# Patch layers of a four-layer image network: the Fourier products cut into 64x64 quarters of the array, and the inverse products in three rounds

## The reference, cut to what matters

```python
t = jnp.einsum('bchw,oc->bohw', x, w_in)                 # 192 -> 192 channels
tp = t.reshape(b, hid, h // 8, 8, w // 8, 8)             # patches of 8x8 pixels
tf = jnp.fft.rfft2(tp, axes=(3, 5)) * fft_filter[None, :, None, :, None, :]
tp = jnp.fft.irfft2(tf, s=(8, 8), axes=(3, 5))
t = conv3x3_depthwise(tp.reshape(b, hid, h, w), w_dw)
x1, x2 = t[:, :hid // 2], t[:, hid // 2:]
out = jnp.einsum('bchw,oc->bohw', gelu(x1) * x2, w_out)  # 96 -> 192 channels
```

## Time and profile before

| what | us |
|---|---|
| three runs, median (lowest to highest) | 2561.39 (2560.28 to 2563.0) |
| the profiled execution's own time | 2555.05 |
| its span, first to last instruction | 2553.0 |
| PE busy in the span | 2232.7 (87%) |
| DVE busy | 1667.8 (65%) |
| ACT busy | 1305.3 (51%) |
| POOL busy | 1113.0 (44%) |

### The profile page before, as it was taken

How to read it: one execution, slowest core, us unless ns; L and a number is a source line. 1 busy time by engine, 2 the same in 40 slices (tenths; PEclk the granted TensorE clock), 3 DMA queues, 4 the chain that set the end, 5 groups by cost and what they waited for, 6 DMA issues and landing times. The chain is left out here.

```text
span 2553.0 us, 63276 instructions
## 1 busy us (share of the span) xinstructions
PE 2232.7 (87%) x22485; PEld 1652.4 (65%) x22612; DVE 1667.8 (65%) x3120; ACT 1305.3 (51%) x2719; POOL 1113.0 (44%) x1393
## 2 busy tenths in 40 slices
PE   0699997998999169999999999999968999789998
PEld 0575645786788047777777777777756656366563
DVE  5345585674575168888888888888863455734557
ACT  0245540084057147777777777777733454334543
POOL 0333150000000147878787878778743222432225
PEclk9999997999999579999999999999989999989999
DMA  8623395415523312222222222222235045950349
GB/s 207 176 78 69 85 330 155 119 31 208 171 41 122 112 42 60 59 59 59 58 60 56 61 56 62 55 61 57 59 87 157 2 89 153 310 165 15 79 123 317
DMA packets 305576, 272.33 MB, mean 107 GB/s; under 512 B 175534, under 2 KB 238798, under 8 KB 299162
## 3 DMA queue, kind: packets, MB, share of 16 engines
q1 hardware_dynamic: 294650, 256.15, 36.1%
q0 software_dynamic: 9280, 6.44, 2.1%
q10 hardware_dynamic: 1496, 7.63, 0.8%
HBM read 165.44 MB, written 81.46 MB: 97 GB/s over the span
## 5 line engine op out<-in xcount | busy, mean ns | idle before, releaser
L1664 DVE TENSOR_TENSOR l_scan_att<-l_scan_decay,l_scan_causal_scores 128x512 f32<-128x512 f32 x384 | 327.4, 853 | 64.2 <-ACT l_scan_decay L1633 64.0
L714 ACT COPY l_arena<-l_body_bank 128x384 f32<-128x384 f32 x192 | 141.3, 897 | 308.3 <-PE l_body_bank L591 308.3
L1627 ACT ACTIVATE l_scan_decay<-l_scan_cum 128x512 f32<-128x512 f32 x384 | 216.3, 597 | 34.4 <-PE l_scan_cum L1519 34.3
L1633 ACT ACTIVATE l_scan_decay<-l_scan_decay 128x512 f32<-128x512 f32 x384 | 227.8, 631 | 4.1
L810 DVE TENSOR_TENSOR l_freq<-l_body_bank,l_filter 128x512 f32<-128x512 f32 x144 | 99.6, 692 | 183.8 <-PE l_body_bank L604 183.8
L1644 ACT ACTIVATE l_scan_yw<-l_scan_y_by_channel,l_scan_norm_b,l_scan_norm_w 128x128 f32<-128x128 f32 x384 | 148.0, 456 | 127.8 <-PE l_scan_y_by_channel L1581 126.8
L1566 PE MATMUL l_scan_gate_projected<-l_scan_xr,l_wf 97*128 97x128 f32 (+1 forms) x1536 | 206.6, 284 | 1.3 <-DVE l_scan_xo L1719 1.2
L1597 PE MATMUL l_scan_gate_projected<-l_scan_yz,l_scan_wo 128*96 128x128 f32 x1536 | 198.5, 279 | 1.1 <-DVE l_scan_yz L1696 1.1
L1597 PEld LDWEIGHTS l_scan_gate_projected<-l_scan_yz,l_scan_wo 128*96 128x96 f32 x1536 | 170.9, 163 | 40.0 <-issue 29.6
L571 POOL TENSOR_TENSOR l_arena<-l_arena 96x512 f32<-96x512 f32 x96 | 122.7, 1278 | 167.2 <-ACT l_arena L779 162.5
L1484 POOL TENSOR_TENSOR l_scan_inter<-l_scan_inter,l_scan_xd 128x384 f32<-128x384 f32 x128 | 128.0, 1000 | 152.5 <-DVE l_scan_inter L1679 152.5
(11 more groups left out here) (193 smaller groups left out, 4995.4 us busy)
## 6 DMA issues: line engine op xcount, KB each, us to landing
l_scan_xc<-convolved_rows SPq DMA_DIRECT2D x128, 224.0 KB, 2.8
x_after<-l_arena SPq DMA_DIRECT2D x64, 384.0 KB, 4.8
l_arena<-x_after SPq DMA_DIRECT2D x64, 384.0 KB, 5.6
convolved_rows<-l_slots SPq DMA_DIRECT2D x48, 441.0 KB
l_conv_x_main<-x_after SPq DMA_DIRECT2D x64, 256.0 KB, 2.6
l_arena<-x_after SPq DMA_DIRECT2D x16, 1024.0 KB, 8.3
prepare_xt<-x SPq DMA_DIRECT2D x8, 1536.0 KB
l_arena<-x SPq DMA_DIRECT2D x32, 384.0 KB, 5.7
```

The costliest lines, as they stand in the source:

```text
L714: nc.scalar.copy(tA[:, b, :, j:j + 2].rearrange("p c q -> p q c"), bank[n % 4][:, 0:2 * C].rearrange("p (q c) -> p q c", q=2)).then_inc(t_ ...
L1627: nc.scalar.activation(decay[:, b % 2, 4 * g:4 * g + 4, :], cum[(b + g) % 2][:], ACT.Relu, scale=-1.0)\
L1633: nc.scalar.activation(group, group, ACT.Exp, scale=-1.0).then_inc(exp_done, 1)
L1664: nc.vector.tensor_tensor(att[:, b, 4 * g:4 * g + 4, :], decay[:, b % 2, 4 * g:4 * g + 4, :], causal[:, b % 2:b % 2 + 1, :].broadcast_to([ ...
```

## The change

The products are made on 64x64 quarters of the array. For the transform, the four quarters are (half h of the block's pixels) x (half c of the channels). Rows h feed bank h of a pair of banks, and columns c are the partitions on which the result lands, so that `freq` now holds the first 96 channels on partitions 0 to 63 and the last 96 on partitions 64 to 127, with the upper and the lower patches of a block side by side in the free dimension: [128, 96, 2 x 128]. A unit is 2 rounds of 4 products of 384 columns in place of 3 products of 512, in the bank pairs 4, 5 and 6, 7 in turn, and DVE filters it in 4 instructions of 384 columns in place of 3 of 512. The filter is loaded in two pieces in the new layout.

The inverse of a group is 3 rounds of 4 products of 512 columns in place of 6 products. A round fills banks 2 and 3 together, and waits for all copies of the round before. DVE and ACT make the same 6 copies each, two a round. In the loop the rounds stand apart: round 0, build(g + 1, 1), round 1, build(g + 2, 0), round 2, and so on DVE and ACT. `gelu`, `gate` and the turning of blocks use the first 128 columns of each channel's 256.

```diff
                 def transform(m):
                     b = m % 2
                     pe.wait_ge(t_copied, (m + 1) * HALF // 2)
-                    for p in range(3):
-                        n = m * 3 + p
-                        if n >= 4:
-                            pe.wait_ge(t_hat, n - 3)
-                        nc.tensor.matmul(bank[4 + n % 4][:], dft, tA[:, b, 64 * p:64 * (p + 1), :].rearrange("p c j -> p (c j)"),
-                                         start=True, stop=True).then_inc(transformed, 1)
+                    for r in range(2):
+                        n = 2 * m + r
+                        if n >= 2:
+                            pe.wait_ge(t_hat, 2 * n - 2)
+                        for c in range(2):
+                            for h in range(2):
+                                at, first = slice(64 * h, 64 * h + 64), CH * c + sets * r
+                                last = nc.tensor.matmul(bank[4 + 2 * (n % 2) + h][64 * c:64 * c + 64, 0:sets * HALF], dft[at, at],
+                                                        tA[at, b, first:first + sets, :].rearrange("p c j -> p (c j)"),
+                                                        start=True, stop=True)
+                        last.then_inc(transformed, 1)
...
-                def invert(g):
-                    for p in range(PIECES):
-                        n = g * PIECES + p
-                        if n >= 2:
-                            pe.wait_ge(own_top, n - 1)
-                            pe.wait_ge(own_low, n - 1)
-                        c = channels(g, p)
-                        nc.tensor.matmul(bank[2 + n % 2][:], idft, freq[:, c:c + 4, :].rearrange("p c n -> p (c n)"),
-                                         start=True, stop=True).then_inc(back, 1)
+                def invert(g, rounds=range(PIECES // 2)):
+                    for q in rounds:
+                        n = g * PIECES // 2 + q
+                        if n >= 1:
+                            pe.wait_ge(own_top, 2 * n)
+                            pe.wait_ge(own_low, 2 * n)
+                        for h in range(2):
+                            for c in range(2):
+                                at, first = slice(64 * c, 64 * c + 64), g * PAIR + 4 * q
+                                last = nc.tensor.matmul(bank[2 + c][64 * h:64 * h + 64, :], idft[at, at],
+                                                        by_slab[at, first:first + 4, :, h, :], start=True, stop=True)
+                        last.then_inc(back, 1)
...
                 for g in range(groups):
                     convolve(g)
+                    if g + 3 < groups:
+                        invert(g + 3, [0])
                     if g + 1 < groups:
                         build(g + 1, 1)
                     if g + 3 < groups:
-                        invert(g + 3)
+                        invert(g + 3, [1])
                     if g + 2 < groups:
                         build(g + 2, 0)
+                    if g + 3 < groups:
+                        invert(g + 3, [2])
...
-                def place(g):
+                def place(g, rounds=range(PIECES // 2)):
                     if g >= STRIPS:
                         dve.wait_ge(convolved, PIECES * (g - STRIPS + 1))
-                    for p in range(PIECES):
-                        n = g * PIECES + p
-                        dve.wait_ge(back, n + 1)
-                        nc.vector.tensor_copy(win[g % STRIPS][0:64, 4 * p:4 * p + 4, 0:NPC:2, 0:NPC],
-                                              bank[2 + n % 2][0:64, :].rearrange("p (c i j) -> p c i j", c=4, i=slabs))\
-                            .then_inc(own_top, 1)
+                    for q in rounds:
+                        dve.wait_ge(back, g * PIECES // 2 + q + 1)
+                        for c in range(2):
+                            first = PAIR * c + 4 * q
+                            nc.vector.tensor_copy(win[g % STRIPS][0:64, first:first + 4, 0:NPC:2, 0:NPC],
+                                                  bank[2 + c][0:64, :].rearrange("p (c i j) -> p c i j", c=4, i=slabs))\
+                                .then_inc(own_top, 1)
...
-            nc.sbuf_tensor(f"{name}_freq", [128, C, H // SLAB * NPC], F32) as freq, \
+            nc.sbuf_tensor(f"{name}_freq", [128, CH, 2 * (H // SLAB) * NPC], F32) as freq, \
...
-        loads = list(pair_loads(arena, flat, 0)) + [(fsym[:], k["filters"][name]), (wi[:, 0], p["w_in"][0:128])]
+        loads = list(pair_loads(arena, flat, 0)) + [(wi[:, 0], p["w_in"][0:128])]
         loads += [(wi[64 * s:64 * (s + 1), 1], p["w_in"][128:C]) for s in range(2)]
+        loads += [(fsym[64 * s:64 * (s + 1)], k["filters"][name][64 * s:64 * (s + 1), CH * s:CH * (s + 1)]) for s in range(2)]
```

More of the change, by code:

```diff
@@ L438, in patch_body @@
     tA = arena[:, n_x:n_x + 2 * n_t].rearrange("p (b c j) -> p b c j", b=2, c=C)
-    by_slab = freq.rearrange("p c (i j) -> p c i j", i=slabs)
+    by_slab = freq.rearrange("p c (i h j) -> p c i h j", i=slabs, h=2)
+    sets = CH // 2
     strips = [arena[:, b * STRIP:(b + 1) * STRIP] for b in range(STRIPS)]
@@ L553, in _ @@
                     pool.wait_ge(rounded, 3)
-                pool.wait_ge(transformed, fills_f)
+                pool.wait_ge(transformed, 2 * units)
                 for b in range(STRIPS):
@@ L655, in _ @@
                 pe.wait_ge(t_copied, fills_a)
-                pe.wait_ge(t_hat, fills_f)
+                pe.wait_ge(t_hat, 4 * units)
                 invert(0)
@@ L744, in gelu @@
                         c = g * PAIR + 4 * p
-                        nc.scalar.activation(freq[:, c:c + 4, :].rearrange("p c n -> p (c n)"), bank[4 + n % 4][:], ACT.Gelu)\
+                        nc.scalar.activation(freq[:, c:c + 4, 0:nblk], bank[4 + n % 4][:].rearrange("p (c n) -> p c n", c=4), ACT.Gelu)\
                             .then_inc(gelu_done, 1)
@@ L755, in _ @@
                     gelu(g)
+                    if g + 3 < groups:
+                        place(g + 3, [0])
                     if g + 1 < groups:
@@ L758, in _ @@
                     if g + 3 < groups:
-                        place(g + 3)
+                        place(g + 3, [1])
                     if g + 2 < groups:
                         matrices(g + 2, 1)
+                    if g + 3 < groups:
+                        place(g + 3, [2])
                 def gather(i):
@@ L806, in _ @@
                         order(m + 2)
[L807 to L808 removed]
+                    for r in range(2):
+                        n = 2 * m + r
                         dve.wait_ge(transformed, n + 1)
[L810 to L813 removed]
+                        for h in range(2):
+                            at = slice(sets * r, sets * (r + 1))
+                            nc.vector.tensor_tensor(by_slab[:, at, 2 * pair:2 * pair + 2, h, QUART * quarter:QUART * (quarter + 1)],
+                                                    bank[4 + 2 * (n % 2) + h][:, 0:sets * HALF].rearrange("p (c s j) -> p c s j", s=2, j=QUART),
+                                                    fsym[:, at].unsqueeze(2).unsqueeze(3).broadcast_to([128, sets, 2, QUART]),
+                                                    ALU.mult).then_inc(t_hat, 1)
                 def matrices(g, f):
@@ L839, in gate @@
                         c = g * PAIR + 4 * p
-                        out = freq[:, c:c + 4, :].rearrange("p c n -> p (c n)")
-                        nc.vector.tensor_tensor(out, bank[4 + n % 4][:], out, ALU.mult).then_inc(gated, 1)
+                        out = freq[:, c:c + 4, 0:nblk]
+                        nc.vector.tensor_tensor(out, bank[4 + n % 4][:].rearrange("p (c n) -> p c n", c=4), out, ALU.mult)\
+                            .then_inc(gated, 1)
                 place(0)
```

16 lines of the change are left out of this document (5 added, 11 removed).

## The result

The changed kernel takes 2525.39 us in the median of four runs (2522.29 to 2528.42), the kernel before 2560.84 in the same comparison: ratio 0.9869, 95% interval 0.9850 to 0.9889. It saves 35 us, where 44.6 were forecast. Faster was right, and 2525 lies in the range of 2500 to 2540; the forecast was 8 us too low.

What follows compares the result with a forecast made beforehand. PE was taken to bound the forward stage, PE and copies to be in balance in the inverse. Forward -49.6, loop -4 and ahead of it +9 sum to -44.6, from 2561.4 to 2517 us; range 2500 to 2540.

Steps and rivals of the forecast that it cites:

- Forward products: Forward stage of the patch layers: quarter products shorten PE's transform, saving 49.6 us in three layers, bounds 44 to 52.
- rival D: Forward stage: ACT binds after all, its copies later by more than 0.4 us; 2538 us, 5 in 100.
- The loop's circle: Inverse in the loop: PE and both banks' copies run one behind the other, 2.49 us a round, step 11.70 for 11.97.
- Rival A: Inverse gains as PE's time falls: a step saves 3 us, x15 = 45, giving 2472 us; 3 in 100.
- B: Quarters overlap only in part, a 512-column set taking 1.73 us: 2616 us; 3 in 100, and 3 for a part.
- The loop's sum: Inverse in the loop: each step gains 0.27 us, x15 steps = -4 us, bounds -6 and +4.
- Rival C: Clock falls in the loop too, 5.1 us a step; 3 in 100 for 9 steps or more, 12 for 2 to 8.
- Ahead of the loop: Inverse rounds before convolve(0): serial rounds and a falling clock cost +3 us a layer, +9 us in all, bounds +1 and +13.
- If it falls after two of the nine rounds: Ahead of the loop: clock falling then starts convolve(0) at 28.3 us, behind PE's own queue, for 24.0: +4.3 us.
- The steps at nothing: Wider channel step of freq in gelu, gate and turn, and the filter's load in two pieces: put at no cost.

Runs made afterwards that it cites:

- The filler's run: Changed kernel plus one unread full-array product of 512 columns behind each of the nine inverse rounds ahead of the loop: 2511.31 us, ratio 0.9806.
- the run with the rings held: Changed kernel with nine rounds ahead of the loop in three bank pairs, ring 1 issued only when ring 0 has landed: 2520.44 us, ratio 0.9853.
- three pairs: Changed kernel with the nine inverse rounds ahead of the loop in three pairs of banks by turns: 2530.82 us, ratio 0.9880.

## Why the prediction was right, and where it was off

**Forward products: right to 0.6 us in 49.6.** The set of four took what I scaled from l1: two sets and a change of form are 1.45 us (1.48 in my terms), and the second change of form is in project, 2.80 for 2.60. ACT did not bind in the units (rival D), though I had read its cover too wide: its copies end 2.63 us after the project (2305.13 + 2.94 against 2305.62 - 0.18), not 2.5, which leaves 0.3 us to spare. At the end the last two transforms were not bound by DVE alone: PE waited for ACT's copies, a wait that I left out, but the end still came in at 5.5 us for 5.2.

**The loop's circle: right.** 11.72 us a step for 11.70, by the same pieces: 1.15 to the copies, 1.29, 0.04. The Trainium skill (TensorEngine Tiling (Array Packing), PSUM Bottleneck) says that tiling speeds up the array and not the copies out of PSUM, which may become the bound. The trace agrees in part: 1.29 of a round's 2.48 us are copies, but PE's 1.15 stand on the same circle, since a round fills both banks. Of what the quarters save on PE, 0.24 us a step is left. Rival A is out, and B too: a set of 512 columns starts its four products within 0.02 us and takes 1.06 to 1.09 us with the start.

**The loop's sum: -0.9 for -4.** Rival C came in part. The clock fell once in the loop of l0 and of l3 and twice in l2; in l3 two steps were 12.61 and 12.41 us, in l2 a fall late in the loop made steps of 12.61 and 9.62 for 11.72 and 7.58. I had priced a fall at 5.1 us; it cost 1.6 to 2.9, for the clock came back sooner than at convolve(0) in the kernel before. The small sum hides two larger terms. The falls cost some 7 us in the three layers (an estimate from the steps over 11.72 and 7.58), and the first steps, with convolve(0) in them, gave about 4 us beyond the circle's 0.24 each: 13.4, 13.0 and 13.4 us for 14.8, 14.6 and 15.1, as the clock was back sooner after convolve(0) had started. The forecast had put both at nothing ("perhaps a little shorter after"). That the two cancel in part is luck.

**Ahead of the loop: the term that was mis-sized, +15.5 for +9, beyond its bound of +13.** The mechanism was as I put it, serial rounds and a lower clock. The step that failed reads "If it falls after two of the nine rounds": it fell after one, in all three layers, so seven rounds took 3.39 us. A round at the low clock was 0.90 us longer, for 0.97 in my terms. With 2.48 + 7 x 3.39 + 1.98 + 0.76 the chain gives 28.9, which is what it shows. And of the +4.3 us that my own sum gave for a fall after two rounds I took only +3; it came to +5.2 on average. The filler's run shows the share: at full clock the stage is 22.3 to 22.9, so the clock is worth 6 us a layer, and the serial rounds alone cost nothing against before, as ring 0 took less time too.

Why it fell after one round stays open. PE had paused for ACT and DVE at the end of the forward stage, which the forecast did not count. But the kernel with forward quarters only has the same pauses and keeps its clock in the full-array products behind them, and the kernel with inverse rounds only is without most of them (PE busy for 5.1 us of the same six) and still lost its clock after one round in two layers, after four in the third. The first line is the end of the forward stage in the changed kernel's l3, the other two are that stretch and the stage ahead of the loop with forward quarters only:

```profile
2321.80:2327.80 6.00, 3.53 (x40) 1.29 (x37) 3.90 (x8) 2.93 (x4) 1.40 (x6) 1.00 0.00 0
```

```profile
2312.40:2318.40 6.00, 3.54 (x40) 1.29 (x36) 3.90 (x8) 2.94 (x4) 1.39 (x6) 1.00 0.00 0
2318.40:2331.00 12.60, 12.38 (x34) 4.81 (x34) 8.72 (x14) 8.05 (x14) 5.62 (x13) 1.00 0.21 43
```

So the rounds take the clock down, with or without those pauses, and after how many of them varies.

**A wrong number that did no harm.** I moved ring 0 with place(0) at a fixed 17.5 us. It took 14.1, 14.2 and 13.4 in the changed kernel, where its followers came later; that this is the reason fits the table of rings and the run with the rings held. As PE's queue bound, the sum didn't use it, which was luck; the two experiments that relied on it (the filler, three pairs) missed.

**The steps at nothing** held: the output stage is the same within 0.1 us and a product of L689 takes 286 ns for 287, so the wider step between channels costs nothing there.

## What to carry to other kernels

Packing products four to a set halves PE's time only where PE is the bound; where a product, its copies and the next product form a circle through the same banks, packing makes a set wait for all its copies, and the time nearly stays (11.72 us a step for 11.96). Price the granted clock with such a change: PE that works in bursts between waits may run at half speed, and then even useless products in the waits can pay (14 us here). And a DMA's time is not its own: what is issued behind it can make it nearly twice as long (22.6 us for 12.5), so that sending the first one early is worth only as much as the followers are kept back.

## What the runs showed of the hardware that was not expected

- Waits of 1.4 us between sets of 1.1 us of quarter products took the clock from 2.4 to 1.2 GHz, after one set in all three layers of the changed kernel and for the other eight; with inverse rounds only it was after one, four and one. The same waits with a full-array product of 512 columns in them did not, with one of 32 columns they did (0.50, 1.00 and 0.52 granted).
- A ring's DMAs took 12.5 to 12.8 us from issue to landing with nothing behind them, and 22.6 to 23.5 us with the DMAs of two more rings behind them.
- A fall of the clock inside the loop cost 1.6 to 2.9 us, against 2.6 to 3.1 for the one at convolve(0) in the kernel before (steps of 14.6 to 15.1 us for 11.96).
